# First expert matrices and tokens as f16 high and low parts instead of four-byte ones

## What is computed

```python
x = x + conv_block(_ln_c(x), ...)            # sign, 2x3 conv, batch norm, relu, sign, conv, batch norm, + input, relu
t = _to_tokens(x)                            # (16, 1024, 64)
t = t + ffn(_ln_t(t), gate_w, gate_b, w1, w2, w3)

def ffn(x, gate_w, gate_b, w1, w2, w3):      # w1, w2: (16, 64, 128); w3: (16, 128, 64)
    probs = softmax(x @ gate_w + gate_b)
    dispatch = top 2 of probs, divided by their sum, else 0
    h1 = einsum('bsd,edh->bseh', x, w1)
    h2 = einsum('bsd,edh->bseh', x, w2)
    hidden = silu(h1) * h2
    expert_out = einsum('bseh,eho->bseo', hidden, w3)
    return einsum('bseo,bse->bso', expert_out, dispatch)
```

## Time and profile before

| | |
|---|---|
| median of 3 runs | 541.8 us (541.31 to 543.06) |
| span of the profiled execution | 598.9 us |
| busy share PE, PEld, DVE, ACT, POOL | 84%, 73%, 74%, 66%, 48% |
| chain that ended last | PE 51%, DVE 17%, ACT 10%, issue 9%, no known releaser 6%, DMA 4% |
| L971 and L973, up matmuls | 588 and 588, mean 310 and 287 ns, each with its weight load of 194 and 195 ns |
| L1004 and L1006, down matmuls | mean 221 and 194 ns, f16 weight loads of 98 ns |
| L703, Silu | 147, mean 609 ns, first at 231.8 us, last at 578.8 us |
| L1513 and L696, token parts | 37 each, median 691 and 608 ns |

### The profile page before, as it was taken

How to read it: one execution, slowest core, us unless ns; L and a number is a source line. 1 busy time by engine, 2 the same in 40 slices (tenths; PEclk the granted TensorE clock), 3 DMA queues, 4 the chain that set the end, 5 groups by cost and what they waited for, 6 DMA issues and landing times.

```text
span 598.9 us, 14226 instructions
## 1 busy us (share of the span) xinstructions
PE 500.9 (84%) x4186; PEld 436.7 (73%) x4186; DVE 441.6 (74%) x1242; ACT 396.0 (66%) x946; POOL 287.9 (48%) x378
## 2 busy tenths in 40 slices
PE   6899997896986627767889899999999999999854
PEld 5566665674764516757878799999998999899753
DVE  4567786685689697556676688888888888888653
ACT  5577885684765303456676588888787878778650
POOL 4000036666667675645555455454444544545351
PEclk9878997996979557879999899999999999999986
DMA  7941101011000012320122221232242425210404
GB/s 295 283 84 36 35 12 61 25 60 62 25 24 29 22 46 66 69 63 21 39 56 57 54 43 39 51 90 54 48 116 49 118 55 147 55 31 17 134 24 141
DMA packets 62664, 40.97 MB, mean 68 GB/s; under 512 B 50003, under 2 KB 54318, under 8 KB 62080
## 3 DMA queue, kind: packets, MB, share of 16 engines
q1 hardware_dynamic: 52208, 23.84, 17.5%
q0 software_dynamic: 8800, 8.94, 4.4%
q10 hardware_dynamic: 1584, 7.29, 3.2%
HBM read 21.46 MB, written 19.19 MB: 68 GB/s over the span
## 4 chain that ended last, share of the span: by engine, by line
PE 51%; DVE 17%; ACT 10%; issue 9%; another core or an unknown queue 6%; DMA 4%; SPq 3%; POOLq 0%; DVEq 0%; ACTq 0%; POOL 0%
PE up L971 9%; PE up L973 8%; PE turn L987 6%; PE up L803 5%; PE lines L1004 5%; PE small L819 3%; ACT xc L703 3%; DVE hidden L1589 2%; DMA x_in<-in_x 2%; PE lines L1006 2%; PE small L848 2%; PE up L789 2%; PE small L952 2%; PE up L778 2%
## 5 line engine op out<-in xcount | busy, mean ns | idle before, releaser
L519 POOL DMA_INDIRECT results<-result,page_in x147 | 154.3, 1050 | 152.0 <-ACT xc L703 103.5
L498 POOL DMA_INDIRECT pages<-payload,slot_int x128 | 127.6, 997 | 141.7 <-DVE slot_int L1414 73.5
L971 PE MATMUL up<-up_w,xs_hi 128*128 x588 | 163.5, 310 | 9.8 <-issue 5.1
L973 PE MATMUL up<-up_w,xs_lo 128*128 x588 | 150.0, 287 | 0.3 <-issue 0.3
L703 ACT ACTIVATE xc<-up 128x512 f32<-128x512 f32 x147 | 89.5, 609 | 76.5 <-PE up L973 48.4
L971 PEld LDWEIGHTS up<-up_w,xs_hi 128*128 128x128 f32 x588 | 114.1, 194 | 16.2 <-issue 13.7
L973 PEld LDWEIGHTS up<-up_w,xs_lo 128*128 128x128 f32 x588 | 114.7, 195 | 0.0
L1589 DVE SCALAR_TENSOR_TENSOR hidden<-up,page_in,xc 128x128 f32<-128x128 f32 x196 | 59.4, 344 | 43.2 <-ACT xc L703 35.4
L1599 DVE TENSOR_TENSOR hidden_lo<-turn,hidden_hi 128x512 f16<-128x512 f32 x98 | 67.0, 684 | 3.9 <-ACT hidden_hi L716 2.8
L987 PE MATMUL turn<-ident,hidden 128*128 128x128 f32 x392 | 60.7, 279 | 2.8 <-DVE branch L1599 1.6
L716 ACT ACTIVATE hidden_hi<-turn 128x512 f16<-128x512 f32 x98 | 60.9, 622 | 3.1 <-PE turn L987 2.5
(11 more groups left out here) (262 smaller groups left out, 999.2 us busy)
## 6 DMA issues: line engine op xcount, KB each, us to landing
pages<-up_w ACTq DMA_DIRECT2D x4, 1332.0 KB, 9.9
page_in<-pages SPq DMA_DIRECT2D x147, 36.0 KB
page_in<-pages SPq DMA_DIRECT2D x147, 32.0 KB
x_in<-in_x SPq DMA_DIRECT2D x7, 512.0 KB
out<-up_raw SPq DMA_DIRECT2D x5, 512.0 KB, 4.8
results<-result,page_in POOLq DMA_INDIRECT x147
up_raw<-in_L_ffn_w SPq DMA_DIRECT2D x4, 512.0 KB, 16.8
pages<-payload,slot_int POOLq DMA_INDIRECT x128
```

Source lines behind the costliest of these rows:

```text
L498: pool.indirect_dma_start(out=pages, out_offset=bass.IndirectOffsetOnAxis(ap=slot_int[q % PAYLOADS][:, t:t + 1], axis=0), in_=payload[q % ...
L519: pool.indirect_dma_start(out=results, out_offset=bass.IndirectOffsetOnAxis(ap=page_in[g % LOADS][:, k, D + AT_TOKEN:D + AT_TOKEN + 1].bit ...
L971: pe.matmul(target, xs_hi[g % 2][:, k * P:(k + 1) * P], weights[:, bass.ds(e * 2, 2 * HID)], start=True, stop=False)
L973: last = pe.matmul(target, xs_lo[g % 2][:, k * P:(k + 1) * P], weights[:, bass.ds(e * 2, 2 * HID)], start=False, stop=True)
```

## The change

The first expert matrices `up_w` and the tokens become f16. `up_w` now has for each expert two blocks, high parts of both matrices and low parts of both, each on all 128 partitions. One tile `xs` takes the place of `xs_hi` and `xs_lo`: high part of a token on partitions 0 to 63, low part on 64 to 127. `up_product` has for each expert still two matmuls of 256 columns, but both with the same stationary matrix, which is the same for all eight of a page; the first takes the high block, the second the low block. Since f16 needs a range, matrices and tokens are scaled by powers of two (`scales` now has four columns, `X_SCALE` is 256) and the scale of the gate half is taken back in the Silu (`back_scales`), that of the other half in the tokens' weights (`weight_scale`). `make_hi(0)` moves from ACT's step 1 to step 4 and waits for the scales, `make_low(0)` from DVE's step 1 to step 5 and covers 128 partitions.

```diff
-        up_w = sb("up_w", [P, E, 2, HID], F32R)
+        up_w = sb("up_w", [P, E, 2, 2, HID], F16)
...
-        xs_hi = [sb(f"xs_hi{i}", [P, CW], F32R) for i in range(2)]
-        xs_lo = [sb(f"xs_lo{i}", [P, CW], F32R) for i in range(2)]
+        xs = [sb(f"xs{i}", [P, CW], F16) for i in range(2)]
...
             def make_hi(m):
-                if m == 0:
+                act.wait_ge(weights_made, WM_SCALES)
+                if m < 2:
                     act.wait_ge(blanked, 64)
-                    act.wait_ge(up_in[0], 32)
-                else:
-                    act.wait_ge(weights_made, WM_SCALES)
-                if m == 0:
-                    act.activation(up_w[:, :, 0, :], up_raw[:, 0, :, :], ACT.Copy).then_inc(hi_made, 1)
-                elif m == 1:
-                    act.activation(up_w[:, :, 1, :], up_raw[:, 1, :, :], ACT.Copy, scale=scales[:, 0:1])\
+                    act.activation(up_w[:, :, 0, m, :], up_raw[:, m, :, :], ACT.Copy, scale=scales[:, 2 + m:3 + m])\
                         .then_inc(hi_made, 1)
...
-                if t == 1:
-                    make_hi(0)
                 if t == 3:
                     make_hi(1)
+                if t == 4:
+                    make_hi(0)
...
-                act.activation(xs_hi[g % 2][:, 0:width], small[:, 0:width], ACT.Copy).then_inc(xs_hi_ready, 1)
+                act.activation(xs[g % 2][:, 0:width], small[:, 0:width], ACT.Copy, scale=X_SCALE)\
+                    .then_inc(xs_hi_ready, 1)
...
-                act.activation(act_s[n % 2].rearrange("p (j h) -> p j h", j=PER_LINE), gates, ACT.Silu)\
-                    .then_inc(silu_done, 1)
+                act.activation(act_s[n % 2].rearrange("p (j h) -> p j h", j=PER_LINE), gates, ACT.Silu,
+                               scale=back_scales[:, 0:1]).then_inc(silu_done, 1)
...
+            act.wait_ge(weights_made, WM_ALL)
             rows_high(0)
...
+                rows = xs[g % 2][:, k * P:(k + 1) * P]
                 for j, e in enumerate(experts):
                     target = up[n % 2][:, 2 * j * HID:2 * (j + 1) * HID]
-                    pe.matmul(target, xs_hi[g % 2][:, k * P:(k + 1) * P], weights[:, bass.ds(e * 2, 2 * HID)],
-                              start=True, stop=False)
-                    last = pe.matmul(target, xs_lo[g % 2][:, k * P:(k + 1) * P], weights[:, bass.ds(e * 2, 2 * HID)],
+                    pe.matmul(target, rows, weights[:, bass.ds(e * 4, 2 * HID)], start=True, stop=False)
+                    last = pe.matmul(target, rows, weights[:, bass.ds(e * 4 + 2 * HID, 2 * HID)],
                                      start=False, stop=True)
...
-                then(dve.tensor_tensor(largest[:, 1:2], largest[:, 0:1], largest[:, 1:2], ALU.mult), 6)
-                then(dve.reciprocal(scales[:, :], largest[:, 1:3]), 7)
-                then(dve.tensor_scalar(scales[:, 0:1], scales[:, 0:1], 2.0 ** 14 / D ** 2, None, ALU.mult), 8)
-                then(dve.tensor_scalar(scales[:, 1:2], scales[:, 1:2], 2.0 ** 14, None, ALU.mult), 9)
+                then(dve.tensor_tensor(tops[:, 0:1], largest[:, 0:1], largest[:, 1:2], ALU.mult), 6)
+                dve.tensor_copy(tops[:, 1:2], largest[:, 2:3])
+                then(dve.tensor_copy(tops[:, 2:4], largest[:, 0:2]), 7)
+                then(dve.reciprocal(scales[:, :], tops[:, :]), 8)
+                then(dve.tensor_scalar(scales[:, 0:1], scales[:, 0:1], 1.0 / D ** 2, None, ALU.mult), 9)
+                then(dve.tensor_scalar(scales[:, :], scales[:, :], HALF_TOP, None, ALU.mult), 10)
...
+                dve.tensor_scalar(x_scales[:, :], scales[:, 2:4], X_SCALE, None, ALU.mult)
...
+                then(dve.reciprocal(unscale[:, 1:2], unscale[:, 0:1]), 13)
+                then(dve.reciprocal(back_scales[:, :], x_scales[:, :]), 14)
+                then(dve.tensor_tensor(weight_scale[:, :], scales[:, 0:1], back_scales[:, 1:2], ALU.mult), WM_ALL)
...
             def make_low(m):
-                dve.wait_ge(hi_made, (1, 3, 2)[m])
-                if m == 0:
-                    dve.tensor_tensor(up_w[D:P, :, 0, :], up_raw[D:P, 0, :, :], up_w[D:P, :, 0, :].bitcast(F32),
-                                      ALU.subtract).then_inc(lo_made, 1)
-                elif m == 1:
-                    dve.scalar_tensor_tensor(out=up_w[D:P, :, 1, :], in0=up_raw[D:P, 1, :, :], scalar=scales[D:P, 0:1],
-                                             in1=up_w[D:P, :, 1, :].bitcast(F32), op0=ALU.mult, op1=ALU.subtract)\
-                        .then_inc(lo_made, 1)
+                dve.wait_ge(hi_made, (3, 2, 1)[m])
+                if m < 2:
+                    dve.scalar_tensor_tensor(out=up_w[:, :, 1, m, :], in0=up_raw[:, m, :, :],
+                                             scalar=scales[:, 2 + m:3 + m], in1=up_w[:, :, 0, m, :],
+                                             op0=ALU.mult, op1=ALU.subtract).then_inc(lo_made, 1)
...
-                dve.tensor_tensor(payload[q % PAYLOADS][:, :, AT_WEIGHT:AT_WEIGHT + PER_LINE], sided[:, :, :],
-                                  by_x[:, :, :], ALU.mult).then_inc(weights_placed, 1)
+                dve.scalar_tensor_tensor(out=payload[q % PAYLOADS][:, :, AT_WEIGHT:AT_WEIGHT + PER_LINE],
+                                         in0=sided[:, :, :], scalar=weight_scale[:, 0:1], in1=by_x[:, :, :],
+                                         op0=ALU.mult, op1=ALU.mult).then_inc(weights_placed, 1)
...
-                dve.tensor_tensor(xs_lo[g % 2][:, 0:width], small[:, 0:width], xs_hi[g % 2][:, 0:width].bitcast(F32),
-                                  ALU.subtract).then_inc(xs_ready, 1)
+                dve.scalar_tensor_tensor(out=xs[g % 2][D:P, 0:width], in0=small[D:P, 0:width], scalar=X_SCALE,
+                                         in1=xs[g % 2][D:P, 0:width], op0=ALU.mult, op1=ALU.subtract)\
+                    .then_inc(xs_ready, 1)
...
                 if t == 1:
                     find_largest(0)
+                if t == 5:
                     make_low(0)
```

19 lines of the change are left out of this document (12 added, 7 removed).

## The result

The changed kernel takes 550.2 us in the median (547.9 to 559.4, 5 runs), beside 541.8 us for the kernel before (540.8 to 543.1). The ratio is 1.013 with a 95% interval of 1.009 to 1.017: slower by some 7 us. The forecast was 536.0, the range ended at 545. Some executions, the profiled one of the changed kernel among them (span 557.7 us), are longer at a lower mean clock (here 0.915 against 0.928 to 0.937); all medians here count them, the ratios leave them out, and I take no sum of the part before the first Silu from such a trace.

A forecast was written before the change was run, and what follows sets the result against it. The prediction took a closed ring of DVE and PE work, 8.26 us per four pages, as the bound: 541.8 - 7.7 (expert stage) + 1.9 (first stage) = 536.0 us. Its own range was 528.5 to 539.4, with rivals up to 545.

The forecast's parts named there:

- The up products: Expert stage: f16 up matmuls start 0.11 us apart, the first included; 0.33 us gained per group of four pages.
- The ring: Expert stage: closed sequence of DVE and PE work between page 2's Silus; 8.26 us per four pages, 8.0 after.
- PE's half: Part of the ring from page 0's down product to page 2's next Silu: 3.99 us, to lose 0.33.
- The Silu: Expert stage, ACT: scale from a tile instead of a constant adds 0.09 us, once per group on the ring.
- Rows of tokens: Expert stage: rows_low on 64 partitions, 0.01 to 0.02 us more by durations, taken as 0; rows_high unchanged.
- The moved preparation: First stage: make_hi(0) moved to ACT's step 4 costs 0.3 us, make_low(0) to DVE's step 5 costs 1.6; together +1.9.
- VectorE's half: Part of the ring from page 2's Silu to page 0's down product: 4.27 us, to grow by the Silu's 0.09.
- PE alone: First rival, expert stage: PE alone sets the pace, all 147 pages gain 0.17 us, giving 518.7 us; chance 0.08.
- The exposed f16 load: Second rival, up products: a page's first matmul distance stays at 0.22 us, giving 541.9 us, no change; chance 0.13.
- The third: Rival, first stage: the moved preparation is fully on the path, 5.3 us in place of 1.9, giving 539.4; chance 0.12.
- the fourth: Rival, slower side: longer PE waits let the clock fall to 1.2 GHz for stretches, 3.7 us a group; chance 0.10.

The follow-up runs named there:

- e3_one_address: Changed kernel with both up products of an expert at one computed address, high and low tokens in two tiles, rows_low on 128 partitions: 534.5 us, ratio 0.986.
- e8_silu_tile: Kernel before with the Silu's scale taken from a tile column of ones: 543.4 us, ratio 1.003.
- e7_all_four: e3_one_address with the Silu's scale as a constant, right for these inputs alone: 532.6 us, ratio 0.987.
- e10_half_low: e7_all_four with rows_low on the upper 64 partitions only, leaving out one product, so its numbers aren't the reference's: 540.8 us, ratio 0.985.
- e1_before: Kernel before, unchanged, run and profiled again: 542.4 us, ratio 1.000.
- e9_fixed_address: Changed kernel with constant addresses for the up products, leaving out the choice of the expert there: 538.1 us, ratio 0.990.
- e4_silu_const: Changed kernel with the Silu's scale as a constant, right for these inputs alone: 548.7 us, ratio 1.011.
- e5_wide_low: Changed kernel with rows_low on 128 partitions on VectorE and ScalarE's high-part copy on 64: 556.2 us, ratio 1.020.

## Why the prediction was wrong

**The step that failed** first is "The up products": "Eight distances go from 1.03 to 1.06 us to 0.88". It took the pitch from the convolution and the down product. The convolution reads fixed addresses. The down product's two matmuls of an expert share a computed one, and their pace of 0.085 us a pair was read in page 1, which has the turning ahead of it; page 0, which comes after a wait, took 0.50 us (463.75 to 464.25), 0.11 to 0.15 a pair in the trace. Neither row has a computation per matmul. The sentence "the count is the same: eight per page" counted matmuls and loads and not what PE's sequencer does for them. The trace of before had the answer in it: 588 computations on L971 and none on L973. Measured: seven distances 0.878 us with two addresses per expert, 0.767 without computations, 0.769 with one. The term of 0.33 us a group on PE's half of the ring came to 0.09 (3.96 to 3.87); without computations it is 0.36 (3.60). Between the changed kernel and the one with fixed addresses lie 13.3 us of stage, 9.4 in the 33 groups.

**The ring** was read rightly. With the pitch as forecast the group should be 8.26 - 0.24 = 8.0 us and the stage 309.1 - 7.7 = 301.4. `e3_one_address` has groups of 7.95 and 8.05 us and halves of 4.33 and 3.63; PE's half is 0.33 under that of before, as forecast. Its 534.5 us stand near 536.0, partly by luck: the forecast less its 1.9 us for the preparation is 534.1. The mechanism was right, for a kernel that was not the one to be run. From `e8_silu_tile` (scale tile and old pitch) to `e3_one_address` the pitch is worth 10.7 us in the 33 groups; the forecast's 0.33 us, without the four of them that have `add_input`, makes 9.6. The lower end of the forecast's own range, 528.5, is 0.3 under what 541.8 - 13 gives; nothing hangs on it.

**The Silu** at +0.09 us, on the ring once per group, was right: 687 ns, and 2.7 us on the kernel before and 3.1 on the changed one in the 33 groups, against 3.0.

**Rows of tokens**, "I take 0", is the second step that failed. It compared durations, of rows on 128 partitions, and 0.69 us against 0.69 was indeed no difference. What counts on the ring is the distance from start to start on both sides, and that grew by 0.15 us at half height: 5.7 us of stage from `e7_all_four` to `e10_half_low`. VectorE's half was to grow by 0.09 for the Silu alone and grew by 0.23 (4.27 to 4.50). No run of the changed kernel measures this step alone.

**The moved preparation**, +1.9 us, was too much: nothing measurable, -2.4 to +0.3, for the move itself. The delay that was counted on VectorE in step 6 did not reach the first Silu, which starts at 210.3 us in `e1_before` and at 208.7, 210.7 and 211.8 in `e3_one_address`, `e9_fixed_address` and `e4_silu_const`. What the move does to the spread of that time is left open: 208.7 to 220.0 us among the profiles with it, 209.3 to 210.8 among the three without.

**The rivals.** PE alone (518.7) fell: with the full pitch gain of `e3_one_address` the time is 534.5, on the ring's value. The exposed f16 load fell: the first distance of a page is that of the others, 0.11 at 464.46, where it had been 0.22. The rule on loads that was weighed there, of the Trainium skill, "TensorE: Matmul & The Clock Gate", section "LDWEIGHTS (loading the stationary operand)", gives 107 ns for each; the loads of `e9_fixed_address` are recorded with 98 ns, and it starts a matmul every 0.11 us with one ahead of each, so they are hidden. The third fell with the moved preparation. In the fourth the side was right and the cause wrong: the clock is 1.00 over the 33 groups. A fifth was missing: one computation per matmul. The count of computations stood in the program and in the trace of before; a sign of their price was page 0's down product in the earlier trace rows.

**The account** goes by the halves of the ring. VectorE's half grew by 0.23 us: 0.06 to 0.09 is the Silu (`e8_silu_tile`, `e4_silu_const`), and 0.17 separates the two f16 kernels that differ in the height of `rows_low` but not in pace (`e9_fixed_address` 4.50, `e3_one_address` 4.33). PE's half fell by 0.09, where 0.36 is there without computations. The rest of the 5.6 us is in single longer groups and in those with `add_input`. The first computation per expert is nearly free (seven distances 0.769 us with it and 0.767 without), as 0.124 us hides behind two matmuls of 0.11 each; the second isn't.

What stays open is how much of the loss comes by a detour. The load of a page's four offsets sits in the same sequencer, normally 0.34 us; in one group of the changed kernel it lay between the wait for the result and the down product. The load is on line L958, in a window of 2 us, and PE's row behind it:

```profile
L958 PEldq TENSOR_LOAD <-roster x1: 1247/1247/1247, 469.2 to 469.2; - x1
```

```profile
470.59 0.23 PE L1006 MATMUL lines<-down_w,hidden_hi 128*128 x1 [0.71 <-DVE result L1623]
```

That group took 8.9 us. Over 240 to 520 us the idle time of the loads before the down product put down to "issue" grew from 9.5 us in `e1_before` to 11.6. Loads of over 0.6 us are as frequent in `e1_before` (4) as here (5). I did not test moving this load. Open too is why the last four pages take 1.6 us longer than in `e1_before`; with fixed addresses they don't.

## What to carry to other kernels

Before a matmul's pitch is forecast, count the distinct run-time addresses, not only the matmuls. Here a computed address with its load takes PE's sequencer 0.124 us, more than a 256-column f16 matmul (0.11 us), and it was computed once for neighbouring matmuls that use the same expression. Lay out data so that the products with one choice share one address, here high over low on the partitions, and the f16 gain comes through (534.5 us instead of 550.2). For a vector step on the path, read the distances from start to start, not its duration. And before a stage is compared between two traces, look at the clock in each part of it: here the first six pages alone made differences of over a microsecond.

## What the runs showed of the hardware

Three things were not expected. A computed address is an instruction of PE's sequencer, 46 ns long, but one per matmul holds the matmuls 0.124 us apart. With four-byte operands (a pitch of 0.119 us before) the second one per expert cost 3.4 us in the 33 groups; in f16, taking out both gave back 9.4 us, and the first was nearly free.

A step on 64 partitions takes as long as one on 128, and it loses the overlap with its neighbours. On VectorE (0.69 us either way) the next step on 128 partitions starts 0.73 us after it instead of 0.61. ScalarE's copy at half height did the same in `e5_wide_low` (0.61 us instead of 0.48).

An f16 load of 98 ns before every 256-column matmul is hidden, while the kernel with the four-byte load of 188 ns had a mean first distance of 0.21 us in a page, 0.09 more than the others.
